# TensorE's semaphore waits in an attention step: redundant ones left out, the others one to an instruction

## The reference, cut to what matters

```python
x = attn_layer(shift_tokens(x), Wqkv[i], q_scale[i], k_scale[i], Wo[i]) + x
x = ffn_layer(shift_tokens(x), ln_g[i], ln_b[i], W1[i], b1[i], W2[i], b2[i]) + x
```

## Time and profile before

| | us |
|---|---|
| median of 3 runs | 2105.45 (2103.52 to 2105.51) |
| the profiled execution's own time | 2106.95 |
| span of the profiled execution | 2105.2 |
| TensorE matmul busy | 2012.3 (96% of the span) |
| VectorE busy | 1548.6 (74%) |
| ScalarE busy | 1398.5 (66%) |
| GpSimd busy | 1226.5 (58%) |
| mean granted TensorE clock | 0.973 of full |

### The profile page before, as it was taken

How to read it: one execution, slowest core, us unless ns; L and a number is a source line. 1 busy time by engine, 2 the same in 40 slices (tenths; PEclk the granted TensorE clock), 3 DMA queues, 4 the chain that set the end, 5 groups by cost and what they waited for, 6 DMA issues and landing times. The chain is left out here.

```text
span 2105.2 us, 84842 instructions
## 1 busy us (share of the span) xinstructions
PE 2012.3 (96%) x32996; PEld 1379.7 (66%) x32996; DVE 1548.6 (74%) x2879; ACT 1398.5 (66%) x4165; POOL 1226.5 (58%) x1376
## 2 busy tenths in 40 slices
PE   7788788999999999999999999999999999999987
PEld 3333233887686776866876767768768677687672
DVE  1498896896786776867967768768678687696763
ACT  4522233886786776857867777678678776686772
POOL 1376773774685554845746756549556566575550
PEclk9888888999999999999999999999999999999998
DMA  1321111211131111221111211112211111121110
GB/s 61 132 70 70 65 55 41 70 43 39 37 91 36 40 45 29 52 76 42 43 39 41 86 37 43 40 33 58 80 37 47 38 41 39 32 53 30 27 29 20
DMA packets 148102, 104.46 MB, mean 50 GB/s; under 512 B 15779, under 2 KB 140257, under 8 KB 146177
## 3 DMA queue, kind: packets, MB, share of 16 engines
q1 hardware_dynamic: 147712, 99.07, 17.0%
HBM read 48.31 MB, written 1.18 MB: 24 GB/s over the span
## 5 line engine op out<-in xcount | busy, mean ns | idle before, releaser
L1382 POOL TENSOR_TENSOR QK<-QK,RN 128x512 f32<-128x512 f32 x384 | 400.2, 1042 | 399.3 <-ACT RN L1115 384.1
L1125 ACT ACTIVATE PR<-ps,MN 128x64 f32<-128x64 f32 x1536 | 356.0, 315 | 162.0 <-DVE MN L1243 147.2
L994 PE MATMUL ps<-W,XS 128*128 128x256 f32 x1536 | 436.3, 407 | 5.1 <-PEq L64 4.1
L1377 POOL TENSOR_TENSOR QK<-PC,PS 128x256 f32<-128x256 f32 x384 | 279.5, 728 | 249.9 <-PE ps L980 245.9
L1151 ACT COPY QKT<-ps 128x512 f32<-128x512 f32 x384 | 224.2, 584 | 247.0 <-PE ps L980 246.9
L1267 DVE TENSOR_REDUCE SS<-SQ 128x8 f32<-128x512 f32 x384 | 260.7, 679 | 59.9 <-ACT SQ L1158 58.8
L994 PEld LDWEIGHTS ps<-W,XS 128*128 128x128 f32 x1536 | 261.5, 190 | 62.1 <-issue 5.4
L1378 POOL TENSOR_TENSOR QK<-PC,PS 128x256 f32<-128x256 f32 x384 | 280.3, 730 | 0.0
L1243 DVE TENSOR_REDUCE MN<-ps 128x4 f32<-128x256 f32 x384 | 162.5, 423 | 140.5 <-PE ps L948 136.6
L1286 DVE TENSOR_TENSOR PC<-ps,TC 128x512 f32<-128x512 f32 x384 | 260.9, 679 | 0.1
L1288 DVE TENSOR_TENSOR PS<-ps,TS 128x512 f32<-128x512 f32 x384 | 260.2, 678 | 0.0
(11 more groups left out here) (137 smaller groups left out, 3222.9 us busy)
## 6 DMA issues: line engine op xcount, KB each, us to landing
V<-V SPq DMA_DIRECT2D x384, 97.5 KB, 2.3
scr<-B_rows SPq DMA_DIRECT2D x32, 512.0 KB, 3.6
V<-V SPq DMA_DIRECT2D x288, 32.5 KB, 2.3
W<-in_Wqkv SPq DMA_DIRECT2D x40, 192.0 KB, 2.9
TC<-in_tcos SPq DMA_DIRECT2D x6, 1024.0 KB, 4.9
TS<-in_tsin SPq DMA_DIRECT2D x6, 1024.0 KB, 8.5
WO<-in_Wo SPq DMA_DIRECT2D x6, 512.0 KB, 4.1
W<-in_W SPq DMA_DIRECT2D x6, 341.0 KB
```

Of the source, the lines that this page charges most:

```text
L994: mm = nc.tensor.matmul(ps[:, par, k * 2 * P:(k + 1) * 2 * P], cols[k], W[:, i, 0:2, :].rearrange("p t m -> p (t m)"), start=True, stop=True)
L1125: e = nc.scalar.activation(PR[:, m % 2, h, slot * DH:(slot + 1) * DH], ps[:, 3 + h, slot * DH:(slot + 1) * DH], ACT.Exp, scale=-1.0, bias= ...
L1377: nc.gpsimd.tensor_tensor(QK[:, par, :, 0:hd], PC[:, par, :, 0:hd], PS[:, par, :, hd:DH], ALU.add)
L1382: nc.gpsimd.tensor_tensor(QK[:, par, :, :], QK[:, par, :, :], bcast_last(RN[:, m // 2 % 2, 8 * par:8 * par + 8], DH), ALU.mult).then_inc(q ...
```

## The change

In the steady passes (`8 <= n < NSTEPS`, 376 of them) all calls of `wait` that another wait already covers are skipped. Those that remain are placed so that each instruction has one:

- QK: `qk` on the first transpose, `pr >= n-5` on the second, `oT >= n-8` on the third. In the kernel before, these two stood ahead of ON's first transpose.
- ON: `on` alone on its first.
- Mask products: `v_sh` on the second. It stood ahead of the values.
- Scores: `pT >= n-6` on the first. It stood ahead of the values.
- Values: `v_cp` on the first.
- V products: `on >= n-6` on the first.
- Transposes of the probabilities: `qkT >= n-3` on the second. It stood in the next pass, ahead of QK and the scores.

No instruction that computes is added, removed or reordered; the diff touches TensorE's stream alone.

```diff
+            def steady(n):
+                return 8 <= n < NSTEPS
...
-                wait(pe, pr, min(n - 5, NSTEPS))
-                wait(pe, oT, m)
+                if not steady(n):
+                    wait(pe, pr, min(n - 5, NSTEPS))
+                    wait(pe, oT, m)
                 pe.wait_ge(on, m + 1)
...
-                wait(pe, pr, m)
-                wait(pe, oT, m - 3)
+                if not steady(n):
+                    wait(pe, pr, m)
+                    wait(pe, oT, m - 3)
+                    pe.wait_ge(qkT, m + 1)
                 for h in range(2):
+                    if steady(n) and h == 1:
+                        pe.wait_ge(v_sh[(n - 7) % 4], 32 * ((n - 7) // 4 + 1))
                     nc.tensor.matmul(ps[:, 3 + h, 0:P], identb[:], MASKB[:, int(s == 0), h, :], start=True, stop=True)
-                pe.wait_ge(qkT, m + 1)
+                if steady(n):
+                    pe.wait_ge(pT, n - 6)
...
-                pe.wait_ge(pT, m + 1)
-                pe.wait_ge(v_sh[m % 4], 32 * (m // 4 + 1))
-                wait(pe, on, m)
+                if not steady(n):
+                    pe.wait_ge(pT, m + 1)
+                    pe.wait_ge(v_sh[m % 4], 32 * (m // 4 + 1))
+                    wait(pe, on, m)
                 wait(pe, v_cp, min(n, NSTEPS))
...
-                wait(pe, qkT, m)
+                if not steady(n):
+                    wait(pe, qkT, m)
                 pe.wait_ge(qk, m + 1)
                 for x in range(2):
                     for k in range(2):
+                        if steady(n) and (x, k) == (0, 1):
+                            pe.wait_ge(pr, n - 5)
+                        if steady(n) and (x, k) == (1, 0):
+                            wait(pe, oT, n - 8)
...
-                wait(pe, v_cp, n)
+                if not steady(n):
+                    wait(pe, v_cp, n)
                 wait(pe, on, n - 6)
...
-                wait(pe, pT, m)
-                wait(pe, on, m)
-                pe.wait_ge(pr, m + 1)
+                if not steady(n):
+                    wait(pe, pT, m)
+                    wait(pe, on, m)
+                    pe.wait_ge(pr, m + 1)
                 for h in range(2):
+                    if h == 1 and 7 <= n < NSTEPS - 1:
+                        pe.wait_ge(qkT, n - 3)
```

## The result

| | us |
|---|---|
| before, median of 4 runs | 2104.48 (2101.33 to 2105.51) |
| after, median of 4 runs | 2083.00 (2081.11 to 2085.18) |
| ratio after to before, with its 95% interval | 0.9899 (0.9885 to 0.9913) |
| the changed kernel once more, on another chip, against before there | 2084.83 to 2108.19, ratio 0.9887 (0.9870 to 0.9905) |
| the profiled execution's own time after, and its span | 2082.23, 2080.4 |

The change saves 21.5 us; the forecast of 2090.0 stood for 15.5. The direction held, and so did the delay on which the forecast rests; the size came out 1.4 times as large.

The account below looks back on a forecast made before the run. TensorE was taken as the bound, its matmuls covering 96% of 2105.2 us, with V products' loads kept waiting. Terms -15.8 + 0.3 = -15.5 us from 2105.45 gave 2090.0 us; range for 8 in 10, 2080 to 2100.

Parts of the forecast that it names:

- The wait for `on` ahead of the V products: V products' first load: delay behind `on` falls from 0.12 to 0.06 us, gaining 15.8 us (bounds 7.5 to 22.6).
- the 0.042 us a pass: Mean gain at the V products, weighing 0.02 us in passes like 57 against 0.06 in passes like 56.
- The values' two separate waits: Two waits ahead of the values: 0.06 us of delay is absorbed before the projection, so gain counted 0.
- The other four: Separate waits in QK, ON, mask products and probabilities' transposes: TensorE's queue is far enough ahead, so removal gains nothing.
- The waits moved forward: Waits asked for earlier are met in quiet passes; 11 passes ahead of a feed-forward cost 0.3 us, up to 2.2.
- Rival A: Values move up and the projection begins under 0.79 behind the scores: 0.06 us a pass, 22.6 us, 2082.5; 22%.
- B: VectorE, with `clamp_pair` in even passes, bounds every other pass: 7.9 us of the gain lost, 2098; 10%.
- C: Second and third QK transposes: each mid-group wait re-arms at 0.06 us, 29 us slower, 2135; 5%.
- D: V products' load: delay stays the same with the wait on itself, nothing measurable, 2105; 5%.

## Why the prediction was right, and what it mis-sized

**The wait for `on` ahead of the V products: right, by mechanism and size.** The delay is 0.06 us in place of 0.12 (medians 54 and 116 ns over all passes), the quiet pass is 3.28 us in place of 3.30, and the part alone gives 16.1 to 16.8 us against 15.8. That it came so close is in part luck: the 0.042 us a pass were weighed from two passes. The 0.02 of the quiet pass lies where the step put it: V products still 0.97 behind the projection, then 0.44 in place of 0.46 to the transposes.

**The values' two separate waits: counted 0, alone they give 6.9 us.** The prediction said that the 0.06 of delay is absorbed, since the projection begins 0.79 behind the scores in both passes, and counted 0. For the projection that is right. But the next consumer of the values is `on`, and the prediction's own rows showed it: in the earlier trace rows `on` ends 582.02 - 580.47 = 1.55 behind the scores with values at 0.32, in the earlier trace rows 578.72 - 577.06 = 1.66 with values at 0.38. It used that 0.11 only to weigh passes like 56 against passes like 57, and dismissed the link with "VectorE takes its minimum over the scores first". The minimum was on time in both; the reciprocal was late. In the whole change this error cost little: the gain overlaps with that of the first part, and taking these two out is worth only 2.0 us outside the eight passes once the others are gone.

**The other four: counted 0, alone they give 5.5 us.** "TensorE's queue far enough ahead" is true of a quiet pass and was read from one. In the trace the gain lies almost wholly in the eight passes during the table loads, which the prediction never looked at. This is the term that the forecast lacked: the whole change gains 5.9 and 6.3 us there, and the V products' wait alone nothing. By size it is the 6 us by which the forecast was too small, though a profiled execution is only one of many. What halts TensorE there stays open.

**The sum.** The parts alone give 16.8 + 6.9 + 5.5 = 29.2 us, the whole 21.5 to 23.4. The last part to be added finds fewer late passes left: the V products' wait is worth 9.3 us on top of the others. Outside the eight passes the trace has 18.0, 8.3 and 1.1 us for the parts and 19.1 for the whole: the first two overlap. A forecast that had added all three would have been too high by 6 to 8 us, about as far off as this one was too low.

**The waits moved forward: right in kind.** Pass 47 after the change:

```profile
527.80 0.42 ACT L1186 COPY PT<-ps 128x256 f32<-128x256 f32 x1
...
528.27 0.30 PEld L957 LDWEIGHTS ps<-QKT 64*32 64x32 f32 x32 [0.17 <-ACT PT L1186]
...
528.54 0.58 PE L976 MATMUL ps<-V,PT 64*32 64x65 f32 x32
...
529.06 1.13 PE L1009 MATMUL ps<-W,XS 128*128 128x256 f32 x4
```

`pT` is done at 528.22, the scores begin 0.05 later, and the projection 529.06 - 528.22 = 0.84 behind `pT`, as the step said (0.06 + 0.79), against 530.57 - 529.75 = 0.82 before. What it left out is that the values come at 0.27 and no longer at 0.63, so `on` comes earlier too: from the projection of such a pass to the next one the 11 passes became 1.03 us shorter in all, while the ones just ahead of them became 0.33 us longer. The 0.33 is the cost that the forecast gave these passes; with the 1.03 behind it they gain on balance.

**The rivals.** Rival A (the values move up too, projection earlier) is half seen: the values do begin earlier, by 0.06 to 0.11 us, and the projection does not. The total, 2083.0, is what rival A gave, 2082.5 (its own 22.6 us make 2105.45 - 22.6 = 2082.9), but for another reason, and its sign, a projection less than 0.79 behind the scores, is absent. By the rule of the Trainium skill, "TensorE: Matmul & The Clock Gate", in its table of specifications, loads are pulled ahead from a queue of 64; the trace agrees in so far as the values' loads begin 0.20 behind the scores, while the scores run. B (VectorE bound in even passes) fell: pass 56 after the change takes 578.46 - 575.18 = 3.28 us like pass 57; the row of its scores:

```profile
575.18 0.46 PE L957 MATMUL ps<-QKT 64*32 64x64 f32 x32
```

C (a wait in the middle of a group re-arms) fell: QK to ON takes 581.32 - 580.88 = 0.44 in pass 57 with two such waits, and the median over all passes is 0.437 in both kernels. D fell with the 0.06.

## What to carry to other kernels

On TensorE's queue, put one wait on each instruction and drop those that another covers, first where the wait ends last: there a lone wait instruction in front delays the work by 0.06 us each time, while elsewhere it may be free. Whether it is free has an edge: ask how far the group can slip before its consumer does, and check every consumer, not only the next group of the same engine. A quiet pass shows the floor; read one disturbed pass beside it, and count how many there are, since a good part of a gain can lie there and parts that share it do not add up. Sum by single passes too: here eight passes of 374 held a quarter of the gain, and a column total had hidden that.

## What the runs showed of the hardware that was not expected

A separate wait instruction whose semaphores are long met takes 51 ns in the records, yet the third and the fourth in a row each moved the next load by 0.11 us. When the wait that ends last rides on the load, the load begins 0.054 us behind the releaser; behind a lone wait instruction it is 0.116.

The time between the last value's product and the reciprocal that reads it is not fixed. In most passes of the changed kernel the reciprocal begins 0.92 us behind the scores, in 57 mostly 0.97 to 1.04, with the starts of scores, values and projection the same. It is more frequent when the values begin late, and not gone when they begin early; then most of the cases, 41 of 57, lie in passes 8 and 10 to 13 of a phase. Its cause is open.

TensorE can stop for 0.6 to 3 us in the middle of a group of equal products with no wait on any of them [pass 70 above]. In these traces it does so almost only in the passes during the loads of the 1 MB tables, when the DMA engines are busy for 0.81 of the time, against 0.23 in an ordinary stretch.
